# Decoder with four layers on one Trainium2 core: front parts of three stages issued within the last steps of the cross attentions ahead of them

## What is computed

```
x = _layernorm(x + _L1_xattn_ref(x, ctx, ctx, ...))   # 16 heads of 8, softmax
x = _layernorm(x + _L1_ffn_ref(x, w_gate, w_up, w_down))
x = _layernorm(x + _L2_attn_ref(...))                 # a selective scan
x = _layernorm(x + _L2_xattn_ref(...))                # rotary, causal, 16 heads of 8
x = _layernorm(x + _L2_ffn_ref(...))                  # attention of 16 heads, then 8 experts, top 2
...
x = _layernorm(x + _L3_xattn_ref(...))                # key mask, 16 heads of 8
x = _layernorm(x + _L3_ffn_ref(x, w_gate, w_up, w_down))
```

## Time and profile before

| | us |
|---|---|
| median of 3 runs | 1792.75 |
| lowest, highest | 1785.6, 1802.65 |
| time of the profiled execution | 1785.0 |
| its span | 1782.9 |
| PE busy | 1545.8 (87%) |
| DVE busy | 1291.4 (72%) |
| ACT busy | 1060.4 (59%) |
| POOL busy | 679.9 (38%) |

### The profile page before, as it was taken

The page is one execution under the profiler, slowest core; times in us unless marked ns, Lnnn a source line. Parts: engine busy times, 40 slices in busy tenths (PEclk is TensorE's granted clock), DMA queues, the critical chain, the costliest instruction groups (busy, mean ns, idle before and its releaser), DMA issues.

```text
span 1782.9 us, 34908 instructions
## 1 busy us (share of the span) xinstructions
PE 1545.8 (87%) x12943; PEld 1106.0 (62%) x12943; DVE 1291.4 (72%) x2876; ACT 1060.4 (59%) x2182; POOL 679.9 (38%) x769
## 2 busy tenths in 40 slices
PE   6488878989998888999988999998989998988875
PEld 5244445768787555677777766665548994655542
DVE  2678854397776888499999677748863448878877
ACT  4388962257665677388899155536763443157755
POOL 3355534588887021356657413320000101501223
PEclk9699988999999999988888999999999999999985
DMA  3200102200000000010000100000000000000000
GB/s 124 108 19 13 36 26 93 68 10 1 1 1 1 2 2 1 4 36 1 1 1 1 57 2 2 2 13 2 2 2 1 1 1 10 1 19 2 2 1 24
DMA packets 14792, 30.95 MB, mean 17 GB/s; under 512 B 1537, under 2 KB 10145, under 8 KB 13857
## 3 DMA queue, kind: packets, MB, share of 16 engines
q1 hardware_dynamic: 13602, 26.63, 4.3%
q0 software_dynamic: 1024, 2.10, 0.4%
HBM read 22.42 MB, written 6.29 MB: 16 GB/s over the span
## 4 chain that ended last, share of the span: by engine, by line
PE 47%; DVE 23%; POOL 10%; issue 9%; ACT 8%; DMA 1%; SPq 0%; DVEq 0%; POOLq 0%; ACTq 0%
PE PS L1324 5%; PE PS L1384 4%; DVE negmax L2628 4%; POOL big L813 4%; PE PS L1641 3%; PE PS L1652 3%; DVE V L3185 3%; POOL big L801 3%; ACT big L2137 2%; PE PS L1406 2%; ACT big L2115 2%; POOL big L809 2%; PE PS L1329 2%; PE PS L1380 2%; PE PS L1398 2%
## 5 line engine op out<-in xcount | busy, mean ns | idle before, releaser
L2115 ACT ACTIVATE big<-PS 128x1024 f32<-128x1024 f32 (+1 forms) x256 | 248.4, 971 | 162.6 <-PE PS L1335 161.7
L2628 DVE TENSOR_REDUCE negmax<-PS 128x4 f32<-128x1024 f32 x192 | 235.0, 1224 | 54.5 <-PE PS L1324 53.4
L697 POOL TENSOR_TENSOR rstd<-veps,mhalf 128x2 f32<-128x2 f32 x72 | 52.0, 722 | 413.6 <-DVE veps L2511 413.2
L1324 PE MATMUL PS<-KS,QS 32*128 32x256 f32 (+1 forms) x1152 | 132.4, 314 | 52.5 <-DVE negmax L2628 38.3
L1324 PEld LDWEIGHTS PS<-KS,QS 32*128 32x128 f32 x1152 | 86.0, 185 | 128.2 <-DVE negmax L2628 89.5
L1384 PE MATMUL PS<-big,V 128*32 128x256 f32 (+1 forms) x2048 | 135.2, 383 | 0.7 <-ACT big L2115 0.4
L1335 PE MATMUL PS<-QS,KS 32*128 32x256 f32 (+1 forms) x1152 | 132.7, 317 | 1.4 <-ACT big L2115 1.4
L723 POOL TENSOR_TENSOR res<-resb,XB 128x256 f32<-128x256 f32 x24 | 17.4, 726 | 271.9 <-ACT resb L2201 271.9
L2647 DVE SCALAR_TENSOR_TENSOR QT<-PS,wint 128x1024 f32<-128x1024 f32 x64 | 77.3, 1220 | 29.9 <-PE PS L1277 29.8
L765 POOL TENSOR_SCALAR KT<-QT 128x1024 f32<-128x1024 f32 x64 | 66.7, 1042 | 68.7 <-DVE QT L2647 66.8
L2280 ACT ACTIVATE QT<-PS,W 128x256 f32<-128x256 f32 x128 | 53.7, 471 | 60.4 <-PE PS L1641 60.4
(11 more groups left out here) (464 smaller groups left out, 4341.0 us busy)
## 6 DMA issues: line engine op xcount, KB each, us to landing
W<-in_wpack SPq DMA_DIRECT2D x1, 4180.0 KB, 12.7
W<-in_wpack SPq DMA_DIRECT2D x1, 2560.0 KB, 9.1
W<-in_wpack SPq DMA_DIRECT2D x1, 2449.5 KB, 8.2
y_rows<-one_more SPq DMA_DIRECT2D x1, 2048.0 KB, 10.9
masks<-in_mask SPq DMA_DIRECT2D x8, 256.0 KB, 2.8
x_rows<-x_tok SPq DMA_DIRECT2D x16, 128.0 KB, 2.1
W<-in_wpack SPq DMA_DIRECT2D x1, 1538.0 KB, 6.0
x_tok<-in_x SPq DMA_DIRECT2D x1, 1024.0 KB, 5.1
```

The source lines that it names most:

```text
L1324: mm = nc.tensor.matmul(PS[:, MAXB[half], o], QS[r, bm % 2, tm, j * P:(j + 1) * P], KS[r, bm % 2, tm, k], start=not a.causal, stop=last)
L2115: nc.scalar.activation(PX[:, T % 2, 2 * p:2 * p + 2, 0:cols], PS[:, exp_banks(g)[0]:exp_banks(g)[0] + 2, 0:cols], ACT.Exp, scale=a.scale). ...
L2628: ins = nc.vector.tensor_reduce(negmax[:, h:h + 2, :].rearrange("p h j -> p (h j)"), banks.rearrange("p h (j k) -> p (h j) k", j=2), AX.X, ...
```

## The change

Three front parts are issued earlier. All edits are in the programs of PE, ACT and DVE, none in SP's or POOL's.

1. **L2f's attention.** `turned_stage` becomes a generator, `turned_steps`, that yields once per step. From step 71 (`AHEAD`) to 78 of L2x, each engine issues one step of L2f, -8 to -1, behind each step of L2x. L2f goes on from step 0. The wait of L2f's first `turn_x` on `t_y_read` is one block less, and the full wait stands at its block 1. DVE waits for L2x's last values before `clear_v`. The fillers inside L2f's steps stay.
2. **L1f.** Within L1x: `gated_turn(0)` and `(1)` at steps 66 and 67, both widens of block 0 at 70 and 71, the first of block 1 and `gated_turn(2)` at 73, `gated_narrow(0)` at 74, the second widen of block 1 and `gated_turn(3)` at 75. In each step they stand behind what L1x does there; so `project(7)` of step 76 stands behind them all. ACT's silu of blocks 0 and 1 is at 71 and 75; DVE's weights and copies at 66 and 67, its product at 73 and 76. PE's loop over b in L1f begins at b = 2.
3. **L3f.** Within L3x: `ternary_turn(0)` at 71, `ternary_widen(0)` at 72, `ternary_turn(1)` at 74, `ternary_widen(1)` at 76 (behind `project(7)`); on ACT copies at 71 and 74, silus at 73 and 77; on DVE `gated(0)` and `quantise(0)` at 74, so ahead of the moments of L3x's block 7. PSUM banks are exchanged.
4. **Fillers.** The three per step end at step 70, and the ten after the loop are gone, for all four stages.

```diff
+AHEAD = 71
             def turned_stage(a):
+                for g in ahead.pop(a.name, None) or turned_steps(a):
+                    if a.name == "L2x" and g >= AHEAD:
+                        if g == AHEAD:
+                            ahead["L2f"] = turned_steps(ATTNS["L2f"])
+                        next(ahead["L2f"])
+            def turned_steps(a):
...
+                    elif n == "L2f":
+                        pe.wait_ge(sem("t_y_read"), before(n, "t_y_read") - 1)
...
+                    if n == "L2f" and b == 1:
+                        pe.wait_ge(sem("t_y_read"), before(n, "t_y_read"))
...
-                        elif g >= PAIRS * B - (8 if a.rope else 0):
-                            stream_on(XB_BANK, 3)
-                if not a.clip and n != "L3x":
-                    stream_on(XB_BANK, 10)
+                        elif PAIRS * B - (8 if a.rope else 0) <= g < AHEAD:
+                            stream_on(FB_BANK if n == "L1x" and g >= 66 else XB_BANK, 3)
+                    if n == "L1x":
+                        gated_ahead(g)
+                    elif n == "L3x":
+                        ternary_ahead(g)
+                    yield g
...
+            def gated_widen(b, k):
+                if b == 0:
+                    pe.wait_ge(sem("wdeq_ready"), 1)
+                    pe.wait_ge(sem("t_probs"), before("L1x", "t_probs") + PAIRS * B)
...
+            def gated_ahead(g):
+                if g in (66, 67):
+                    gated_turn(g - 66)
+                elif g in (70, 71):
+                    gated_widen(0, g - 70)
+                elif g == 73:
+                    gated_widen(1, 0)
+                    gated_turn(2)
+                elif g == 74:
+                    gated_narrow(0)
+                elif g == 75:
+                    gated_widen(1, 1)
+                    gated_turn(3)
...
+            def ternary_ahead(g):
+                if g == 71:
+                    ternary_turn(0)
+                elif g == 72:
+                    ternary_widen(0)
+                elif g == 74:
+                    ternary_turn(1)
+                elif g == 76:
+                    ternary_widen(1)
...
+                    if n == "L1x" and g in (71, 75):
+                        gated_silu(g // 75)
...
+                        if n == "L2f":
+                            dve.wait_ge(sem("t_values"), at("t_values", 0))
                         clear_v(0)
...
+                            elif g == PAIRS * B + 10:
+                                ternary_gated(0)
+                                ternary_quantise(0)
...
+            def gated_ahead(g):
+                if g == 66:
+                    gated_weights()
+                    gated_copy_x(0)
+                elif g == 67:
+                    gated_copy_x(1)
+                elif g == 73:
+                    gated_product(0)
+                    gated_copy_x(2)
+                elif g == 76:
+                    gated_product(1)
+                    gated_copy_x(3)
```

More of the change, by code:

```diff
@@ new lines, in gated_narrow @@
+            def gated_narrow(b):
+                pe.wait_ge(sem("L1f_h"), b + 1)
+                if b >= 2:
+                    pe.wait_ge(sem("var"), before("L1f", "var") + b - 1)
+                for j in range(2):
+                    for c in range(3):
+                        mm = nc.tensor.matmul(PS[:, (OUTB, FB_BANK)[b % 2], j * P:(j + 1) * P], QT[:, 3 + c, j * P:(j + 1) * P],
+                                              wdeq[:, 768 + c * P:896 + c * P], start=c == 0, stop=c == 2)
+                mm.then_inc(sem("y"), 1)
@@ L1723, in turn @@
[L1723 to L1760, removed]
+                for b in range(2, B):
+                    gated_widen(b, 0)
+                    gated_narrow(b - 1)
                     if b == 2:
                         scan_turn_x(0)
-                    widen(b, 1)
+                    gated_widen(b, 1)
                     if b + 2 < B:
-                        turn(b + 2)
+                        gated_turn(b + 2)
@@ L1773, in L1f @@
                 scan_inputs(0)
[L1774 removed]
+                gated_narrow(B - 1)
                 scan_inputs(1)
@@ L2099, in wide_stage, with turned_steps @@
                         copy_fold()
+            ahead = {}
             def turned_stage(a):
+                for g in ahead.pop(a.name, None) or turned_steps(a):
+                    if a.name == "L2x" and g >= AHEAD:
+                        if g == AHEAD:
+                            ahead["L2f"] = turned_steps(ATTNS["L2f"])
+                        next(ahead["L2f"])
+            def turned_steps(a):
                 n, rows = a.name, min(P, a.vcols)
@@ new lines, in gated_residual, with gated_weights @@
+            def gated_residual(b):
+                dve.wait_ge(sem("y"), before("L1f", "y") + b + 1)
+                dve.wait_ge(x_done, base["L1f"] + b)
+                line.step(nc.vector.tensor_tensor(res[:, :, :], both(PS[:, (OUTB, FB_BANK)[b % 2], 0:S]), x_tok[:, 2 * b:2 * b + 2, :], ALU.add))
+                moments(line, None)
+            def gated_weights():
+                dve.wait_ge(sem("wint_loaded"), 16)
+                nc.vector.tensor_scalar(wdeq[:, :], wint[:, :], 1.0 / 127.0, None, ALU.mult).then_inc(sem("wdeq_ready"), 1)
@@ L3142, in L1f @@
[L3142 to L3149 removed]
+                gated_residual(0)
+                for b in range(2, B):
+                    gated_residual(b - 1)
+                    gated_product(b)
```

224 lines of the change are left out of this document (121 added, 103 removed).

## The result

The changed kernel takes 1782.7 us in the median of 20 runs (1779.3 to 1795.1), the kernel before, run beside it, 1794.3 us in 20 runs (1783.1 to 1802.7). The ratio is 0.9943, with a 95% interval of 0.9925 to 0.9961: 10.2 us less (7.0 to 13.5). A second comparison gave 0.9954 (0.9932 to 0.9976), 8.2 us less. So the change is a small gain, within 1%.

A forecast was written before the change was run, and what follows sets the result against it. No engine bounds the whole: the chain leads over PE for 47% and DVE for 23%, so each stage border was priced. +1.2 + 1.5 - 4.6 - 3.7 - 1.4 = -7.0 us gave a median of 1785.7 us, range 1776 to 1797.

The forecast's parts named there:

- L1f, relay: L1x to L1f: front work in PE's queue delays `project(7)` by 5.3 us and `residual(0)` by 1.2; +1.2 us.
- L1f, clock: L1f: PE's new standstill of about 6.5 us makes the next dense work start at low clock; +1.5 us, between 0 and 3.
- L2f: L2x to L2f: earlier first transposes and zeroing let `maximum(0)` begin at 1197.2 in place of 1201.8; -4.6 us.
- L3f: L3x to L3f: `narrow(0)` comes 5.2 us earlier, `subtract(2)` at about 1739.2 instead of 1742.94; -3.7 us.
- fillers at L2f's end: End of L2f's attention: without its 19 fillers the router's product starts sooner; -1.4 us, bounds -1.5 and +2.
- VectorE's queue decides: Start of L2f: DVE's zeroing, then L2x's last moments, set when `maximum(0)` begins, 1197.2 in place of 1201.8.
- from block 2 on DVE decides: L3f: DVE's queue limits the gain from block 2 on, so `subtract(2)` comes only 3.7 us earlier.
- without them it starts at 1343.9: -1.4: End of L2f: with the fillers gone, the router's product starts at 1343.9 instead of 1345.35; -1.4 us.
- An absorbed front: Rival, L1x to L1f: last block's relay isn't held up, `residual(0)` gains 4.1 us; -13.8 in all, 1778.9 us; chance 0.20.
- Not relieved: Rival, L2f and L3f: old and new relays hold each other up and the gains vanish; 1794.1 us; chance 0.15.
- Low clock throughout L1f: Rival, L1f: clock stays low after the standstill, 25 us of PE work takes twice that; 1809.3 us; chance 0.04.
- No effect: Rival, all three borders: a moved wait isn't met before the tail ends, only the fillers go; 1791.3 us; chance 0.09.

The follow-up runs named there:

- L1f_undone: The changed kernel with L1f's front part put back behind L1x on all three engines and the fillers of L1x's end restored; ratio to the kernel before 0.9983.
- relay_first: The changed kernel with L1f's front part still moved ahead, but behind what L1x's last block needs of PE and DVE; ratio to the kernel before 0.9939.

## Why the prediction was right, and where not

The forecast was -7.0 us, 1785.7 for the median, and the likeliest case; measured were -10.2 (-13.5 to -7.0) and, a second time, -8.2, with medians inside the range. By its terms, with what the traces of all the kernels give:

| term | predicted | measured |
|---|---|---|
| L1f, relay | +1.2 | +0.1 |
| L1f, clock | +1.5 | +1.9 at L2a's first scan, +0.1 at its last sum |
| L2f | -4.6 | -4.8 |
| L3f | -3.7 | -4.6 |
| fillers at L2f's end | -1.4 | +1.0 |
| sum | -7.0 | -8.2 |

That the sum came so near is in part luck: the first four terms came out 1.1, 1.4, 0.2 and 0.9 us lower than predicted, and the last 2.4 higher.

- *L1f, relay.* `project(7)` was predicted 5.3 us later and came 5.0 later. But the relay from there to the end of the layer norm was taken as unchanged, and it took 748.69 - 743.26 = 5.4 us instead of 6.3. In before, DVE turned the weights to float beside it. Of the 0.85 us, 0.44 are of POOL's small product (1.15 before, 0.71 after) and 0.36 a wait of DVE between its two statistics. These are rows of before:

```profile
735.30 0.75 DVE L3143 TENSOR_SCALAR big<-wint 128x1152 f32<-128x1152 int32 x1
735.47 1.15 POOL L697 TENSOR_TENSOR rstd<-veps,mhalf 128x2 f32<-128x2 f32 x1 [1.55 <-DVE veps L2511]
```

  The product took 1.15 us in the four traces in which this conversion stands beside it, `L1f_undone` among them, and 0.71 in the ten others. It goes with the conversion; by what means isn't shown, since the conversion was never moved alone. So the layer norm came 4.1 us later, and the slack of `residual(0)` was just that: 14.61 us behind L1x's last values, against 14.50.
- *L1f, clock.* The mechanism and its place were as predicted (a standstill of 6.4 us, then half the clock), and so nearly was its size. That it comes back wasn't foreseen. L2a's first three scan intervals sum to 21.8 us in before and 20.3 in after; with the standstill filled it is 21.7 again. There are 10.2 us of low clock in them in before and with the standstill filled, and 6.8 in after. So it isn't the head start of a queue, but the clock that falls at other moments. Why the one low stretch spares another stays open.
- *L2f.* Right in size and in each step: transposes, zeroing 4.0 behind, moments behind the zeroing. Only that VectorE's queue decides is half the truth; TensorE's first scores lie 0.3 us behind it.
- *L3f.* Right in mechanism: `narrow(0)` gains 5.2 us, and later blocks less. The step "from block 2 on DVE decides" priced DVE's work 0.7 too high: `subtract(2)` comes 4.4 us earlier and not 3.7 (the prediction's own `gated(2)`, 1735.5 in place of 1739.0, gives 3.5), and the span ends 4.6 earlier, averaged over four traces without and ten with the front part (65.27 and 60.70).
- *Fillers.* The term that failed. The step "without them it starts at 1343.9: -1.4" priced the queue nearly rightly (the router starts 1.6 to 1.9 us sooner, and 1.8 are left at equal low clock) and put the clock at nothing in the sum, leaving it to the bounds, +2 at the most. It took back 2.8 on average. The mean of +1.0 lies within the bounds; the longest traces without the fillers (139.2) are 2.8 above the shortest with them (136.4).
- *Rivals.* An absorbed front (-13.8) needed `project(7)` on time: refuted by the 5.0 us. `relay_first` shows that another order can reach its price: its local terms (-6.1, -4.8, -4.6, +1.0) sum to -14.5, and its ratio gives -10.9 (-16.6 to -5.2). Not relieved: the intervals in L2f and L3f both shrank. Low clock throughout L1f: it lasted one stretch of 6.8 us. No effect: refuted by the two intervals that went back when L2f and L3f were put back.
- *What stays open.* Local terms give -8.2 and lie within both measured intervals. The rest of the -10.2 is not a better clock over the whole: the mean granted clock was 0.933 in the changed kernel's first 20 runs and 0.935 in the next 12, against 0.936 in the 35 runs of the kernel before beside these. For the first comparison the clocks of the kernel before aren't known, so whether those 2 us are chance stays open.

## What to carry to other kernels

Work moved ahead into the tail of a stage belongs behind the instructions of that tail which others wait for; the same 7 us of matmuls gained nothing in front of the last block's relay and 6.1 us behind it. A filler on TensorE is to be priced twice, by its time in the queue and by the clock of what follows; here the second was the larger. Short matmuls behind a weight load each follow the clock as well. When unchanged code ahead of the change differs by 12 us between executions, compare intervals between landmarks over several traces, and set the times of runs against their mean clocks before trusting a difference of a few microseconds.

## What the runs showed of the hardware

- The router's 32 products, 8 columns each behind a weight load of 128, took 3.64, 4.29, 5.35 and 6.99 us at a mean granted clock of 1.00, 0.83, 0.67 and 0.50. Time multiplied by clock is 3.5 to 3.6 each time. The weight loads fill the stretch as the matmuls do (PEld 7.00 of 7.00), so both follow the granted clock; one load is listed with some 0.19 us at 2.4 GHz and 0.33 at 1.2, overlapping the next.
- At L2f's end, between the last values and the router, PE did 2.6 to 2.9 us of work in pieces in 4.4 to 4.7 us in the traces without fillers. From there to L3a the clock was low for 6.9 to 13.7 us. With 6.1 us of work in 6.3 it was low for 3.4 to 6.8.
- POOL's product on 128x2 took 1.15 us in the four traces in which DVE turned 128x1152 integers to float beside it, and 0.71 in the other ten.
- The way to L1x's last values, the same code in all but its last 7 us, took 726.6 to 738.6 us over 14 traces, with 65 to 106 us of them at 1.2 GHz. Over whole runs, 0.01 less of mean granted clock went with 12.2 us more.
